# Constant products in four more waits of TensorE in a four-layer network kernel

## The reference

```python
    x = L0_attn_x
    xn = _layernorm(x, axis=-1)
    s = _L0_attn_ref(xn, ...)
    g = _silu(_L0_ffn_ref(xn, ...))
    x = x + s * g
    ...
    xn = _layernorm(x, axis=-1)
    s = _L2_attn_ref(xn, ...)
    g = _silu(_L2_ffn_ref(xn, ...))
    x = x + s * g
    xn = _layernorm(x, axis=-1)
    s = _L3_attn_ref(xn, ...)
    g = _silu(_L3_ffn_ref(xn, ...))
    x = x + s * g
```

## Time and profile before

| what | value |
|---|---|
| runs | 4200.03, 4197.98, 4192.66 us; median 4197.98 us |
| profiled execution | 4196.52 us, with a span of 4193.1 us and 3.4 us around it |
| mean granted TensorE clock | 0.939 |
| PE busy | 3506.4 us, 84% of the span |
| DVE busy | 2530.1 us, 60% |
| ACT busy | 1823.9 us, 43% |
| POOL busy | 821.5 us, 20% |
| L96, constant products | 427.9 us in 1576 matmuls |

### The profile page before, as it was taken

How to read it: one execution, slowest core, us unless ns; L and a number is a source line. 1 busy time by engine, 2 the same in 40 slices (tenths; PEclk the granted TensorE clock), 3 DMA queues, 4 the chain that set the end, 5 groups by cost and what they waited for, 6 DMA issues and landing times. The chain is left out here.

```text
span 4193.1 us, 55509 instructions
## 1 busy us (share of the span) xinstructions
PE 3506.4 (84%) x19466; PEld 1814.7 (43%) x19615; DVE 2530.1 (60%) x5500; ACT 1823.9 (43%) x3753; POOL 821.5 (20%) x721
## 2 busy tenths in 40 slices
PE   3988798888988889887988889888898879888867
PEld 1444444444344444454444443444434544444434
DVE  3566655666556655666556665566556665566655
ACT  1544444444443535444444444444354444444414
POOL 1023300331012400233003310124002230033114
PEclk9999999999999999999999999999999999999978
DMA  4000111001011010000111010110200001110130
GB/s 155 25 17 26 36 30 34 31 4 61 5 34 34 1 65 25 17 26 32 34 34 31 4 63 4 34 34 1 65 28 14 27 36 30 34 31 4 63 84 21
DMA packets 87847, 140.06 MB, mean 33 GB/s; under 512 B 12472, under 2 KB 62466, under 8 KB 85002
## 3 DMA queue, kind: packets, MB, share of 16 engines
q1 hardware_dynamic: 81042, 127.30, 9.5%
q10 hardware_dynamic: 6522, 9.06, 0.7%
HBM read 106.14 MB, written 29.39 MB: 32 GB/s over the span
## 5 line engine op out<-in xcount | busy, mean ns | idle before, releaser
L618 DVE TENSOR_REDUCE nmax<-banks 128x1 f32<-128x512 f32 (+3 forms) x1216 | 761.1, 658 | 392.5 <-PE banks L440 228.2
L538 ACT ACTIVATE probs<-banks 128x512 f32<-128x512 f32 (+3 forms) x1024 | 475.7, 526 | 302.9 <-PE banks L458 299.9
L440 PE MATMUL banks<-ks,qs 72*128 72x512 bf16 (+3 forms) x1536 | 464.1, 348 | 98.3 <-DVE nmax L618 68.3
L458 PE MATMUL banks<-qs,ks 74*128 74x512 bf16 (+3 forms) x1536 | 461.9, 338 | 41.2 <-ACT probs L538 17.2
L96 PE MATMUL banks<-filler,identb 128*128 128x512 bf16 x1576 | 427.9, 392 | 36.0 <-PEq L76 26.5
L440 PEld LDWEIGHTS banks<-ks,qs 72*128 72x128 bf16 x1536 | 144.0, 101 | 418.4 <-DVE nmax L618 246.2
L538 ACT ACTIVATE early<-banks 128x256 f32<-128x256 f32 (+3 forms) x512 | 198.1, 440 | 196.6 <-PE banks L458 196.6
L1295 ACT ACTIVATE probs<-banks,nm 128x192 f32<-128x192 f32 x512 | 172.6, 422 | 229.9 <-DVE nm L1247 229.9
L501 PE MATMUL banks<-probs,v 128*32 128x512 f32 (+3 forms) x2048 | 239.1, 539 | 32.4 <-POOL probs L584 22.9
L253 POOL TENSOR_TENSOR rstd<-var,neghalf 128x4 f32<-128x4 f32 (+1 forms) x16 | 21.2, 1324 | 1246.2 <-DVE var L204 1137.8
L96 PEld LDWEIGHTS banks<-filler,identb 128*128 128x128 bf16 x1712 | 171.5, 101 | 205.0 <-issue 63.5
(11 more groups left out here) (453 smaller groups left out, 6528.2 us busy)
## 6 DMA issues: line engine op xcount, KB each, us to landing
qs<-parts_scratch SPq DMA_DIRECT2D x300, 96.0 KB
ks<-parts_scratch SPq DMA_DIRECT2D x288, 96.0 KB
parts_scratch<-parts SPq DMA_DIRECT2D x50, 384.0 KB, 2.5
shared<-in_w_h SPq DMA_DIRECT2D x17, 1024.0 KB, 7.6
shared<-in_w SPq DMA_DIRECT2D x25, 256.0 KB, 4.0
qs<-max_parts SPq DMA_DIRECT2D x192, 4.0 KB
xn<-in_x SPq DMA_DIRECT2D x9, 256.0 KB, 2.7
factor_scratch<-g SPq DMA_DIRECT2D x9, 256.0 KB, 2.2
```

What stands on the lines that cost most here:

```text
L440: mm = nc.tensor.matmul(K.ps[:, b, i * keys:(i + 1) * keys], K.qs[0:72, 4 * g + j, t * P:(t + 1) * P], K.ks[0:72, 4 * g + j, 0:keys], star ...
L458: nc.tensor.matmul(K.ps[:, b, q0:T], K.ks[0:KR, h, k * P:(k + 1) * P], K.qs[0:KR, h, q0:T], start=True, stop=True).then_inc(scored2, 1)
L538: nc.scalar.activation(probs[:, 4 * (q % QUADS) + m % 4, q0:T], K.ps[:, bank("second", m), q0:T], ACT.Exp, scale=scale).then_inc(exped, 1)
L618: nc.vector.tensor_reduce(nmax[:, t, h:h + len(heads)], K.ps[:, n % 2, 0:len(heads) * keys].rearrange("p (j k) -> p j k", k=keys), AX.X, A ...
```

## The change

It adds `keep_busy` in four places of TensorE's list, and nothing else; the numbers are matmuls for one iteration:

- each local attention (two calls): 4 products into bank 7 behind `scores(1)`, and 5 behind `scores(2)`, ahead of `turn(0)`;
- third attention, q = 15: 5 products ahead of the last weighing, behind a wait for 62 of the 64 exponentials, into the bank of second scores 61, and 7 behind the weighing;
- gated norm: 12 products into bank 7 ahead of the four transposes.

```diff
@@ -490,6 +491,9 @@
                         if waits_first and s > 8 * NG + 1:
                             keep_busy(nc, K, 0, 10 if q == 4 * NG - 1 else 2)
+                        if beside.LAST_FILLERS and q == 4 * NG - 1:
+                            pe.wait_ge(exped, 4 * q + 2)
+                            keep_busy(nc, K, bank("second", 4 * q + 1), beside.LAST_FILLERS[0])
                         if causal:
                             pe.wait_ge(masked, q + 1)
@@ -502,6 +506,8 @@
                         mm.then_inc(weighed, 1)
+                        if beside.LAST_FILLERS and q == 4 * NG - 1:
+                            keep_busy(nc, K, bank("second", 4 * q + 1), beside.LAST_FILLERS[1])
@@ -1226,9 +1232,12 @@
                 scores(0)
                 scores(1)
+                keep_busy(nc, K, 7, 4)
                 for w in range(UNITS):
                     if w + 2 < UNITS:
                         scores(w + 2)
+                    if w == 0:
+                        keep_busy(nc, K, 7, 5)
                     turn(w)
@@ -1459,6 +1468,7 @@
     KEEPS_BUSY = False
+    LAST_FILLERS = 5, 7
@@ -1809,6 +1819,7 @@
         yield self.NORM + 1
+        keep_busy(nc, K, 7, 12)
         for t in range(NT):
             pe.wait_ge(self.xn_ready, t + 1)
```

More of the change, by code:

```diff
@@ L349 @@
     FILLED = {}
+    LAST_FILLERS = None
     started = False
```

## The result

The changed kernel takes 4144.24 us (median of four runs, 4141.75 to 4146.06), the kernel before beside it 4196.69 us (four runs, 4192.66 to 4200.03). The profiled execution took 4146.06 us with a span of 4142.2 us; the mean granted clock rose from 0.939 to 0.963.

A forecast was written before the change was run, and what follows sets the result against it. The prediction saw TensorE waiting at the four places and losing time to its lowered clock. Gains of 5.9 + 14.4 + 17.9 = 38.2 us, less 6.8 and 7.6 given back, left 23.8: 4174.2 us, range 4152 to 4192.

The forecast's parts named there:

- LA1: First local attention, eight iterations: 293.6 us before, forecast to gain 5.9 us by running at full clock.
- NORM: Gated norm's transposes to the experts' barrier, eight iterations: 75.2 us before, forecast to gain 17.9 us.
- C: Rival: new products do not raise the clock, run at half and overrun their waits; 32 us slower, 4230 us; chance 0.06.
- END: Third attention's last weighing to the second local attention, eight iterations: 104.7 us before, forecast to gain 14.4 us.
- E: Rival: the products hide in their waits but the clock falls all the same; 4198 us; chance 0.03.
- D: Rival: every microsecond of low clock costs half of one; gain at most 82 us, 4116 us; chance 0.02.
- LA2: Second local attention, eight iterations: 287.8 us before, forecast to lose 6.8 us to half clock behind its barrier.
- TH: Third attention up to its last weighing, eight iterations: 695.1 us before, forecast 0, bounds -20.9 and +3.0 us.
- ATT: Attentions of layers 0 and 1 and `prepare`, seven iterations: 1706.0 us before, forecast 0.
- FF: Stretch from the second local attention to the gated norm's transposes, eight iterations: 200.0 us before, forecast 0.
- EXP: First work of the experts, behind their barrier, eight iterations: 28.9 us before, forecast to lose 7.6 us.
- A: Rival: the clock is gained at the changed places and lost nowhere else; 38 us gained, 4160 us; chance 0.24.

The follow-up runs named there:

- third alone: Kernel before plus only the constant products around the third attention's last weighing: 4188.70 us against 4192.40, ratio 0.9988.
- the change + 8: Changed kernel plus 8 constant products ahead of the first local attention's first scores, where nothing covers them: 4169.51 us, ratio 0.9936 to the kernel before.
- Local alone: Kernel before plus only the constant products of both local attentions: 4210.77 us against 4192.40, ratio 1.0043.
- first local attention alone: Kernel before plus the local attentions' constant products in the first call only: 4206.44 us against 4192.05, ratio 1.0030.
- norm alone: Kernel before plus only the gated norm's twelve constant products: 4185.74 us against 4192.40, ratio 0.9984.
- before + 8: Kernel before plus 8 constant products ahead of the first local attention's first scores: 4197.93 us against 4194.58, ratio 1.0001.

## Why the prediction was wrong

**The sign and two terms were right.** LA1 gained 5.8 of 5.9 us, NORM 18.0 of 17.9, and both do so in every run that has their products, but for NORM where ten products hold the experts' barrier. The products stand 0.22 us apart and hide in their waits, so C falls; in one second local attention (iteration 0) four of them run at half clock, 1.67 us, and overrun as C said. The clock is held at LA1, END and NORM in all iterations, so E falls. D wanted 82 us.

**A term was mis-sized: the third attention's end**, 14.4 us forecast and 21.6 measured. Two steps failed. One is "From their start to L1173 is 3.92 us, which by the code DVE's three additions and the barrier set". DVE and the barrier need 3.27 us from the copy on; in the earlier trace rows it was 4.01, because the closing products, begun at half clock, ended at 947.37 and held the barrier. The run without them shows this. That adds 3.6 us in eight. The other is "so the mean gain is 0.28 less". The chain up to the copy is the same 9.36 us in all eight iterations; iteration 1 was longer than the mean only behind it, in those closing products, so nothing was to be taken off. The chain gave 2.25 us an iteration, 18.0 in eight, where 2.08 had been read and 1.8 were counted: the other 3.6 us.

**The give-back ahead of the second local attention** was sized too high. PE now idles 1.67 us there and not 2.2, by the same step, and a low clock meets LA2 in iteration 0 alone (36.92 us at clock 0.95): +0.9 us where 6.8 were forecast. That the shorter wait is the reason is not shown: with the same 1.67 us, third alone pays 1.5 us in four iterations of eight and the change + 8 pays 0.8 us in four. A low clock in half of the iterations, as forecast, does occur; which of them pay differs from version to version. The price of 1.7 us was too high, 0.8 to 1.0 us where the products are there.

**The experts' barrier** gave back 5.3 us where 7.6 were forecast. "Three more iterations" at 5.20 us was wrong in form: all eight pay, each for a part. The reason given, the length of the wait, does not decide alone, as the two iterations of before show.

**What failed beyond sizes is the sum itself**, the step "38.2 - 6.8 - 7.6". For the third attention's long stretch the prediction says "I take 0", and for the other untouched stretches it has no term. They gave 7.3 us (TH), 4.4 (ATT) and 1.2 (START), and took 1.6 (FF). Together with END 7.2, LA2 5.9 and EXP 2.3 us, that is the 27 us between the 23.8 of the forecast and the 50.9 of the span. The experiments show that this is no remainder: the three parts alone come to 8 us slower, together to 52 us faster, and pairs of them to 20 to 44 us faster. The bounds of -20.9 and +3.0 for TH were near (680.9 to 700.6 us over all runs, so -14.2 to +5.5), but the range took only a part of the gain in. A named the right direction, its 38 us with nothing given back, but not the reason: something was given back, and more gained where nothing was touched.

**The rule weighed.** END ran about 13.37 x 0.38 x 2 = 10.2 us at half clock in iteration 1 of before, and at full clock the stretch is 2.99 us shorter, the late closing products included: three tenths. The Trainium skill's "TensorE: Matmul & The Clock Gate", section Terms, would have half. At EXP, where PE never waits, 5.20 against 2.66 us, its rule holds.

**What stays open.** Why TH, ATT and START gave 12.9 us in the change is not shown beyond their clock: the profiles show where it was low, not what set that. Which pattern a version falls into could not be told from one trace, and the runs do not show how to foretell it. Local alone and first local attention alone also spread from run to run (4197 to 4219 us and 4184 to 4221 us), while the change stays within 4.3 us; that each execution reaches the loop at another moment would fit, but was not shown. No version that makes the clock independent of the moment was tried.

## What to carry to other kernels

Where PE's clock falls in short waits, take the waits that follow one another through a loop together, and judge the set as a whole: a part measured alone can read slower (here +18 us) and still be worth 25 to 29 us in the set. Compare whole iterations, and the stretches that the edit does not touch, before you add up gains place by place. And look at what a barrier waits for by its last arrival: the constant products that were to keep the clock up can themselves be late when they run at half of it (up to 0.8 us an iteration here).

## What the runs showed of the hardware

In some versions the loop settles. Iterations of identical work come out at 481.2 to 481.3 us in the change from its third on, at 488.0 to 488.2 in norm alone, at 491.3 to 491.6 in first local attention alone, and alternate between 480.1 and 482.5 in the version with six products at the experts. In others the length neither stays nor alternates: 482.5 to 492.2 in the kernel before, 481.5 to 486.5 with ten products at the experts. The difference lies in which stretches get a low clock: 2.66 or 5.20 us behind one barrier, 84.3 or 87.9 us for a third attention. That a delay of 1.7 us an iteration can be free (before + 8) or cost well over its length (the change + 8) fits this, and had not been expected.
